# Seven passes of a two-layer kernel in one block, semaphores counted on over the passes

## The chip, the cores and the metric

The kernel runs on one core of one Trainium2 chip. The metric is the device time of one execution in microseconds; it is repeated, and the median stands for the kernel.

## The reference

Sixteen samples of 512 tokens by 256 channels, f32, go through two layers with adaptive layer norm (shift, scale and gate per sample, from a small product with the conditioning vector):

```python
mod = (_silu(L0_c) @ L0_wmod).reshape(L0_c.shape[0], 6, 1, -1)
h = _layernorm(x) * (1 + ca) + sa
x = x + ga * _L0_attn_ref(h, ...)      # 16 heads, q/k layer norm, causal softmax
h = _layernorm(x) * (1 + cb) + sb
x = x + gb * _L0_ffn_ref(h, ...)       # silu(w1 x)*(w2 x), two 1024x1024 gelu stages, w3
# layer 1, its own c and wmod
x = x + ga * _L1_attn_ref(h, ...)      # in-projection, selective scan over 512 steps, 16 states
x = x + gb * _L1_ffn_ref(h, ...)       # blocks of 32 rounded to an fp6 grid, one 256x256 product
```

## The kernel before

The work is a software pipeline over samples. A **pass** `b` has up to four parts with a flag each: `att` and `ffn` (layer 0's attention and feed-forward of sample `b`), `pre` (layer 1 of sample `b-1`: in-projection, then states 0 to 11 of the selective scan) and `fin` (sample `b-2`: the last four states, "tail", the gate, the output projection, the quantised product and the store). Passes 2 to 15 have all four and are one body in a loop `nc.Fori(2, B)`; passes 0, 1, 16 and 17 are written out around it. Pass 0 is cut in two (its attention, then a block that finds a flag, then its feed-forward, the "feed").

One pass is one call of `one_block` (L479): a block with one list of calls for each engine, interleaved by hand. TensorE, VectorE (DVE), ScalarE (ACT), GpSimd (POOL) and SyncE (SP, which loads weight tiles) meet at a block's end. After it `turn_over` (L2012) is a second block, in which POOL clears all semaphores, so each pass can count from zero; then the engines meet again and, in the loop, branch back.

```python
def one_pass(b, att, fin, pre, has_rest):
    one_block(b, att, fin, pre, att, has_rest)
    if att or pre:
        turn_over()
```

The end and the start of a pass, which the prediction speaks of:

- End, in this order on DVE: the last scan steps (L1694, L1703), `ffn_add` (L1724, reads the last product of the feed-forward), `next_scale` (L225: multiplies the centred next sample `ln_x` by its reciprocal deviation). On ACT: square, Ln, Exp of the next sample's layer norm, then `rotate_b` (L1285, copies `xa` to `xb`). On POOL: the last eight scan sums (L590). On PE: the last feed-forward product, then `next_var` (L214).
- Start: DVE `pick_mod` (L1603: copies this pass's columns of `mod` to `m0`, `m1`, `m2`; L1607 and L1610 two tiny products), then `tail_in` (L1622) and `tail_scan` (L1631), then `normalise` (L1750) for the first q/k tile. ACT `att_norm` (L1193, needs `m0` and the scaled `ln_x`, writes `h_ln`), four `tail_decay` (L1202), then `square` (L1316) of the first projection. PE `tail_spread` (L728), `pre_mean` (L208, reads `xb`), `project` (L840, reads `h_ln`). POOL `clear` (L531 to L536): a memset of two columns, of `v_pad` (128x2048), of `row_max` (128x1024), and of the ones column.

PE also carries, for each product with a weight tile, a branch over code for the weights' rounding rest (L783).

Of the kernel before, what the change touches and what calls it, by code (L numbers as in the profile page):

```python
# [40 lines left out]
SA, CA, GA, SB, CB, GB = (DC * i for i in range(6))  # L41


def build(nc, a, y_fm, x2_store=None):
    B = a["x_fm"].shape[0] - 1
    ctx = ExitStack()
    with ctx:
# [111 lines left out]
        def bank(i):  # L159
            return ps[:, i, :]  # L160
# [50 lines left out]
        def pe_var(pe, k, bk):  # L211
            pe.wait_ge(ln_sq, k)
            for c in range(DC):
                mm = pe.matmul(bank(bk), mean_mat[:, :], ln_s[:, c, :], start=(c == 0), stop=(c == DC - 1))  # L214
            mm.then_inc(ln_var, 1)

        def dve_centre(dve, src, k, bk):
            dve.wait_ge(ln_mean, k)
            if k > 1:
                dve.wait_ge(ln_out, DC * (k - 1))  # L220
            dve.tensor_tensor(ln_x[:, :, :], src[:, :, :], bcast_c(bank(bk)), ALU.subtract).then_inc(ln_cent, 1)  # L221

        def dve_scale(dve, k):
            dve.wait_ge(ln_rstd, k)
            dve.tensor_tensor(ln_x[:, :, :], ln_x[:, :, :], bcast_c(ln_s[:, 1, :]), ALU.mult).then_inc(ln_norm, 1)  # L225

        def act_square(act, k):
            act.wait_ge(ln_cent, k)
            if k > 1:
                act.wait_ge(ln_norm, k - 1)  # L230
            act.activation(ln_s[:, :, :], ln_x[:, :, :], ACT.Square).then_inc(ln_sq, 1)

        def act_rstd(act, k, bk):
            act.wait_ge(ln_var, k)
            act.activation(ln_s[:, 0, :], bank(bk), ACT.Ln, bias=eps[:, 0:1]).then_inc(ln_log, 1)
            act.wait_ge(ln_log, k)
            act.activation(ln_s[:, 1, :], ln_s[:, 0, :], ACT.Exp, scale=-0.5).then_inc(ln_rstd, 1)

        def act_affine(act, dst, k, m, scale, shift):
            act.wait_ge(ln_norm, k)  # L240
# [238 lines left out]
        def one_block(b, att, fin, pre, ffn, has_rest, first=False):  # L479
            numbers = iter(range(1, 5))  # L480
            k_pre, k_fin, k_ffn, k_next = (next(numbers) if on else None for on in (pre, fin, ffn, ffn))

            def heads_of(quad):
                return [quad // 2 * HC + 2 * g + quad % 2 for g in range(4)]

            def pair_of(v, h):
                return v[:, 2 * h:2 * h + 2, :]

            def at_of(n, m):
                return IM * (n - HEAD) + m  # L490

            def wait_tile_used(sp, r):
                if r < HM // 2:
                    sp.wait_ge(up_done, 2 * (r + 1))
                else:
                    sp.wait_ge(mid_done, r - HM // 2 + 1)

            with nc.Block() as block:
                @block.sync
                def _(sp):  # L500
                    if first:
                        split_sync(sp)
                    elif att:
                        first_tiles(sp)
                    if ffn:
                        sp.wait_ge(att_added, DC)
                        sp.dma_start(xn[:, :, :], a["x_fm"][b + 1]).then_inc(x_loaded, 16)
                        if pre:
                            sp.wait_ge(acc_init, IM)
                            sp.wait_ge(u_ready, 2)  # L510
                        with sp.If(has_rest > 0):
                            for r in range(2):
                                sp.dma_start(wrest[:, r, :].bitcast(F32), w_lo[r]).then_inc(rest_loaded[r], 16)
                        for r in range(3, FT):
                            wait_tile_used(sp, r - 3)
                            sp.dma_start(wring[:, r % 3, :].bitcast(F32), w_hi[r]).then_inc(w_loaded[r % 3], 16)
                            with sp.If(has_rest > 0):
                                if r == 3:
                                    wait_tile_used(sp, 0)
                                    sp.dma_start(wrest[:, 0, :].bitcast(F32), w_lo[2]).then_inc(rest_loaded[0], 16)  # L520
                                wait_tile_used(sp, r - 2)
                                sp.dma_start(wrest[:, r % 2, :].bitcast(F32), w_lo[r]).then_inc(rest_loaded[r % 2], 16)
                        sp.wait_ge(x_loaded, 16)
                    if fin:
                        sp.wait_ge(stored, 16)

                @block.gpsimd
                def _(pool):
                    def clear():
                        if fin or pre:  # L530
                            pool.memset(hb[:, 4:8, :].rearrange("p (a b) t -> p a b t", b=2)[:, :, 1, 0:1], 0.0).then_inc(tail_cols, 1)  # L531
                        if att:
                            pool.memset(v_pad.rearrange("p a b c -> p (a b c)"), 0.0).then_inc(pads_clear, 1)
                            pool.memset(row_max.rearrange("p a b c -> p (a b c)"), 0.0).then_inc(pads_clear, 1)
                            pool.wait_ge(pads_clear, 1)
                            pool.memset(v_pad[:, :, :, HS:HS + 1], 1.0).then_inc(ones_set, 1)  # L536

                    def causal_probs(quad, u):
                        if att:
                            for j, at in T_GROUPS[u]:  # L540
                                pool.wait_ge(exp_done, 3 * quad + u + 1)
                                blk = probs[u][:, :, at:at + P]
                                pool.affine_select(blk, blk, [[0, 4], [1, P]], ALU.is_ge, 0.0, base=0, channel_multiplier=-1).then_inc(p_masked, 1)  # L543

# [1581 lines left out]
```

## Time and profile before

| | us |
|---|---|
| median of 3 runs | 4514.94 (4514.47 to 4517.28) |
| the profiled execution's own time | 4515.7 |
| span in its trace (first to last instruction) | 4513.9 |
| busy: PE / DVE | 3731.1 / 3552.5 |
| busy: POOL / ACT | 2517.6 / 2436.1 |
| mean granted TensorE clock | 0.909 of full speed |

"Busy" counts the time in which an engine executes. The idle time in brackets on a timeline's line is that of the engine just before the line's work, with the work that seems to have ended it; "issue" means that the profile shows nothing waited for, and names ending in q are sequencers.

### The profile page before, as it was taken

To read this page: it belongs to the slowest core of one execution; us is meant where nothing else is said; L and a number is where in the kernel's file an instruction comes from. 1 tells how busy PE (TensorE), PEld (TensorE's weight loads), DVE (VectorE), ACT (ScalarE), POOL (GpSimd) and SP (SyncE) were. 2 spreads that over 40 slices of the span, in tenths; PEclk is the share of its full clock that TensorE was granted. 3 is DMA by queue.
4 is the path that set the end of the run, shared out by engine and by line. 5 is a ranking of instruction groups with operands and counts; after the bars stand their busy time and mean duration, and the time that the engine had idled before them with its cause. 6 is when DMAs were issued, how large, how long until landed. Compare 5 with 4: busy or idle time off the path is not lost. (4 is left out here: it accounts for less than half of the span.)

```text
span 4513.9 us, 51258 instructions
## 1 busy us (share of the span) xinstructions
PE 3731.1 (83%) x17261; PEld 2207.2 (49%) x17261; DVE 3552.5 (79%) x3917; ACT 2436.1 (54%) x3413; POOL 2517.6 (56%) x1895
## 2 busy tenths in 40 slices
PE   5788888889888888989888888989888888888623
PEld 3364645546464544636464554646455464645301
DVE  4514788888897888888787887879788888978895
ACT  2343555656465555646565564656555564655532
POOL 0132747557483746648474664848375574837562
PEclk8697999999999999999999999999999999999856
DMA  5530201102020211203020120303011020202000
GB/s 180 215 103 1 90 19 57 57 22 92 5 94 15 77 37 33 80 5 108 1 91 23 47 66 10 104 1 99 15 61 52 24 90 5 94 15 80 19 5 5
DMA packets 69414, 247.75 MB, mean 55 GB/s; under 512 B 9600, under 2 KB 10112, under 8 KB 68736
## 3 DMA queue, kind: packets, MB, share of 16 engines
q1 hardware_dynamic: 66816, 235.28, 15.6%
q10 hardware_dynamic: 2304, 8.39, 0.5%
q8 instruction: 204, 3.34, 0.3%
q14 instruction: 90, 0.74, 0.1%
HBM read 212.19 MB, written 31.46 MB: 54 GB/s over the span
## 5 line engine op out<-in xcount | busy, mean ns | idle before, releaser
L590 POOL TENSOR_TENSOR kept<-kept,hb 128x512 f32<-128x512 f32 x640 | 809.7, 1303 | 28.2 <-DVE hb L1703 28.2
L558 POOL TENSOR_TENSOR kept<-kept,hb 128x1024 f32<-128x1024 f32 x128 | 335.6, 2639 | 766.9 <-DVE hb L1638 694.2
L1694 DVE TENSOR_TENSOR_SCAN hb<-ps,hb 128x512 f32<-128x512 f32 x640 | 742.8, 1206 | 6.5 <-ACT ps L1227 5.6
L794 PE MATMUL ps<-hid_bhi,wring 128*128 128x512 f32 x1536 | 623.5, 406 | 17.3 <-issue 13.8
L794 PE MATMUL ps<-hid_blo,wring 128*128 128x512 f32 x1536 | 607.7, 396 | 0.0
L1227 ACT ACTIVATE ps<-kept,a_neg 128x512 f32<-128x512 f32 x640 | 431.6, 691 | 263.6 <-DVE hb L1694 263.5
L1764 DVE TENSOR_REDUCE room<-ps 128x4 f32<-128x2048 f32 (+3 forms) x256 | 375.7, 1489 | 251.3 <-PE ps L962 250.1
L543 POOL TENSOR_SCALAR_AFFINE_SELECT room<-room 128x512 f32<-128x512 f32 x256 | 224.4, 893 | 586.2 <-ACT room L1389 586.2
L794 PE MATMUL ps<-hid_ahi,wring 128*128 128x512 f32 x1280 | 514.3, 402 | 18.8 <-POOL hid_alo L605 18.4
L794 PE MATMUL ps<-hid_alo,wring 128*128 128x512 f32 x1280 | 503.5, 393 | 0.0
L1389 ACT ACTIVATE room<-ps 128x2048 f32<-128x2048 f32 (+1 forms) x192 | 305.2, 1590 | 257.7 <-PE ps L988 257.7
L1703 DVE TENSOR_TENSOR hb<-hb,ps 128x512 f32<-128x512 f32 x640 | 402.7, 677 | 16.3 <-PE ps L757 16.3
L794 PEld LDWEIGHTS ps<-hid_bhi,wring 128*128 128x128 f32 x1536 | 290.6, 189 | 118.3 <-DVE ln_s L1718 19.4
L794 PEld LDWEIGHTS ps<-hid_blo,wring 128*128 128x128 f32 x1536 | 290.6, 189 | 66.1 <-issue 3.3
L1683 DVE TENSOR_TENSOR hb<-kept,ps 128x512 f32<-128x512 f32 x480 | 306.8, 679 | 18.2 <-POOL kept L590 8.6
L960 PE MATMUL ps<-room 32*128 32x512 f32 (+3 forms) x2048 | 232.5, 526 | 71.0 <-DVE room L1771 23.6
L794 PEld LDWEIGHTS ps<-hid_ahi,wring 128*128 128x128 f32 x1280 | 240.5, 188 | 103.1 <-POOL hid_alo L605 43.5
L1631 DVE TENSOR_TENSOR_SCAN hb<-hb 128x1024 f32<-128x1024 f32 x128 | 288.9, 2279 | 1.0 <-issue 0.8
L988 PE MATMUL ps<-room 32*128 32x512 f32 (+3 forms) x2048 | 215.3, 518 | 70.4 <-DVE room L1764 54.6
L794 PEld LDWEIGHTS ps<-hid_alo,wring 128*128 128x128 f32 x1280 | 240.6, 188 | 53.1 <-issue 0.2
L757 PE MATMUL ps<-bc_parts,bc_sel 128*128 128x512 f32 x320 | 137.6, 463 | 125.5 <-DVE hb L1683 77.2
L728 PE MATMUL ps<-bc_parts,bc_sel 128*128 128x512 f32 x128 | 81.1, 633 | 172.8 <-issue 119.1
(188 smaller groups left out, 7710.7 us busy)
## 6 DMA issues: line engine op xcount, KB each, us to landing
wring<-w_hi SPq DMA_DIRECT2D x352, 512.0 KB, 3.3
kept<-in_wffn SPq DMA_DIRECT2D x22, 512.0 KB, 5.3
w_hi<-wring SPq DMA_DIRECT2D x22, 512.0 KB, 6.2
w_lo<-wrest SPq DMA_DIRECT2D x22, 512.0 KB, 3.7
xn<-in_x_fm SPq DMA_DIRECT2D x17, 512.0 KB, 3.3
out_fm<-xc ACTq DMA_DIRECT2D x16, 512.0 KB, 6.8
room<-in_wmod SPq DMA_DIRECT2D x2, 1536.0 KB, 8.1
win<-in_win SPq DMA_DIRECT2D x1, 1024.0 KB, 8.4
```

What stands on the lines that cost most here:

```text
L543: pool.affine_select(blk, blk, [[0, 4], [1, P]], ALU.is_ge, 0.0, base=0, channel_multiplier=-1).then_inc(p_masked, 1)
L558: pool.tensor_tensor(pair_of(acc, h), pair_of(acc, h), pair_of(hb, h), ALU.add).then_inc(tail_acc, 2)
L590: pool.tensor_tensor(acc[:, m, :], acc[:, m, :], hb[:, s % 8, :], ALU.add).then_inc(acc_done, 1)
L794: mm = pe.matmul(bank(bk), wring[:, r % 3, at + k * P:at + (k + 1) * P], src[i][:, k, :], start=(k == 0 and i == 0), stop=(k == K - 1 and ...
L960: pe.matmul(bank(g)[:, at:at + w], q_ver[r, p, c, i * P:(i + 1) * P], k_ver[r, p, c, 0:w], start=True, stop=False)
L1227: act.activation(bank(2 + m % 2), dt[:, m, :], ACT.Identity, bias=1.0, scale=a_neg[:, m, n:n + 1]).then_inc(a_ready, 1)
L1389: act.activation(probs[u], ps[:, 0:4, 0:G_WIDTH[u]], ACT.Exp).then_inc(exp_done, 1)
L1631: dve.tensor_tensor_scan(both, pair_of(hb, 2 + h).rearrange("p a t -> p (a t)"), both, 0.0, ALU.mult, ALU.add).then_inc(tail_scanned, 2)
L1683: dve.tensor_tensor(hb[:, s % 8, :], u[:, m, :], bank(0), ALU.mult).then_inc(b_ready, 1)
L1694: dve.tensor_tensor_scan(hb[:, s % 8, :], bank(2 + m % 2), hb[:, s % 8, :], 0.0, ALU.mult, ALU.add).then_inc(scanned, 1)
L1703: dve.tensor_tensor(hb[:, s % 8, :], hb[:, s % 8, :], bank(1), ALU.mult).then_inc(y_ready, 1)
L1764: ins = dve.tensor_reduce(cols, ps[:, 0:4, at:at + (i + 1) * P], AX.X, ALU.max, negate=True)
```

## The change

`one_block` becomes five functions, one for each engine, which take a pass as a record with the passes in front of it in the same block. `run(passes)` opens one block, and each engine goes through all the passes of the list. A target of a wait is counted on by what earlier passes of the block add to that semaphore (`since`). Where the block's end used to order two passes, waits are added at the place of first use. The lists of calls inside a pass stay in their order. The loop now has two turns of seven passes; the feed and pass 1 share a block, and so do passes 16 and 17. `turn_over` stays after each block except the last. SP's waits for the input load and the store move to the block's end.

```diff
+        def counting(p):
+            def since(signal, n):
+                earlier = 0
+                for q in p.before:
...
+                        flag, count = per_pass[signal.num]
+                        earlier += count * {"att": q.att, "ffn": q.ffn, "pre": q.pre, "fin": q.fin}[flag]
+                return earlier + n
...
+            elif att:
+                sp.wait_ge(mid_done, since(mid_done, 0))
                 first_tiles(sp)
...
             def clear():
                 if fin or pre:
+                    pool.wait_ge(acc_done, since(acc_done, 0))
                     pool.memset(hb[:, 4:8, :].rearrange("p (a b) t -> p a b t", b=2)[:, :, 1, 0:1], 0.0).then_inc(tail_cols, 1)
                 if att:
+                    pool.wait_ge(mid_done, since(mid_done, 0))
                     pool.memset(v_pad.rearrange("p a b c -> p (a b c)"), 0.0).then_inc(pads_clear, 1)
...
             def pre_mean():
                 if pre:
+                    pe.wait_ge(rotated, since(rotated, 0))
+                    pe.wait_ge(ln_cent, k_pre.number - 1)
...
             def tail_spread(which, j):
...
+                    else:
+                        pe.wait_ge(ffn_added, since(ffn_added, 0))
+                        pe.wait_ge(gelu_done, since(gelu_done, 0))
+                        pe.wait_ge(head_y, since(head_y, 0))
...
             def att_norm():
                 if att:
+                    act.wait_ge(ln_norm, sum(q.pre + q.fin + 2 * q.ffn for q in p.before))
+                    act.wait_ge(hid_split, since(hid_split, 0))
+                    act.wait_ge(mid_done, since(mid_done, 0))
...
             def pick_mod():
+                dve.wait_ge(ln_out, DC * sum(q.pre + q.fin + q.ffn for q in p.before))
+                dve.wait_ge(ffn_added, since(ffn_added, 0))
+                dve.wait_ge(out_ready, since(out_ready, 0))
+                dve.wait_ge(att_added, since(att_added, 0))
...
             def tail_in(j, h):
...
+                    else:
+                        dve.wait_ge(acc_done, since(acc_done, 0))
...
+        def run(passes):
+            with nc.Block() as block:
+                @block.sync
+                def _(sp):
+                    for p in passes:
+                        sync_pass(sp, p)
+                    for p in passes:
+                        finish(sp, p)
...
-        one_block(0, False, False, False, True, has_rest)
-        turn_over()
-        one_pass(1, True, False, True, has_rest)
-        with nc.Fori(2, B) as b:
-            one_pass(b, True, True, True, has_rest)
-        one_pass(B, False, True, True, has_rest)
-        one_pass(B + 1, False, True, False, has_rest)
+        feed = Pass(0, False, False, False, True, False, ())
+        whole_0 = Pass(0, True, False, False, True, False, ())
+        run([feed, Pass(1, True, False, True, True, False, (whole_0,))])
+        turn_over()
+        with nc.Fori(0, (B - 2) // 7) as turn:
+            steady = []
+            for i in range(7):
+                steady.append(Pass(turn * 7 + (2 + i), True, True, True, True, False, tuple(steady)))
+            run(steady)
+            turn_over()
+        last = Pass(B, False, True, True, False, False, ())
+        run([last, Pass(B + 1, False, True, False, False, False, (last,))])
```

DVE before, from the end of a pass (pass 1, the loop's first pass behind it) over the boundary:

```order
L225 TENSOR_TENSOR ln_x<-ln_x,ln_s 128x1024 [waits ln_rstd]
L498 UNCONDITIONAL_BRANCH
L2051 UNCONDITIONAL_BRANCH [waits barrier_Pool_Activation_PE_DVE_SP_release]
L1590 UNCONDITIONAL_BRANCH
L1603 ISA
L1603 COPY m<-mod 128x12
L1603 ISA
L1603 COPY m<-mod 128x12
L1603 ISA
L1603 COPY m<-mod 128x12
L1607 TENSOR_TENSOR g<-m,s 128x2 [waits mod_ready]
L1610 TENSOR_TENSOR gbias<-m,ffb 128x2
```

DVE in the changed kernel, at the boundary between two passes of one block:

```order
L228 TENSOR_TENSOR ln_x<-ln_x,ln_s 128x1024 [waits ln_rstd]
L1719 ISA [waits out_ready,att_added,ffn_added,ln_out]
L1719 COPY m<-mod 128x12
L1719 REGISTER_ALU
L1719 COPY m<-mod 128x12 x2
L1723 TENSOR_TENSOR g<-m,s 128x2 [waits mod_ready]
L1726 TENSOR_TENSOR gbias<-m,ffb 128x2
L1740 TENSOR_TENSOR hb<-kept,ps 128x1024 [waits tail_b,acc_done,mod_ready]
```

The three branches and the wait for the other engines are gone; `pick_mod`'s copies stand right behind `next_scale`, with waits on signals of other engines in front.

POOL before, the same boundary (L2017 is the clearing of the semaphores):

```order
L590 TENSOR_TENSOR kept<-kept,hb 128x512 [waits y_ready,acc_done] x8
L498 UNCONDITIONAL_BRANCH
L2015 UNCONDITIONAL_BRANCH [waits barrier_Pool_Activation_PE_DVE_SP_gather]
L2017 ISA
L2014 UNCONDITIONAL_BRANCH
L2051 UNCONDITIONAL_BRANCH [waits barrier_Pool_Activation_PE_DVE_SP_gather]
L527 UNCONDITIONAL_BRANCH
L531 MEMSET hb 128x2
L533 MEMSET room 128x2048
L534 MEMSET room 128x1024
L536 MEMSET room 128x64 [waits pads_clear]
```

POOL in the changed kernel:

```order
L668 TENSOR_TENSOR kept<-kept,hb 128x512 [waits y_ready,acc_done] x8
L608 MEMSET hb 128x2 [waits acc_done]
L611 MEMSET room 128x2048 [waits mid_done]
L612 MEMSET room 128x1024
L614 MEMSET room 128x64 [waits pads_clear]
L636 TENSOR_TENSOR kept<-kept,hb 128x1024 [waits tail_y] x2
```

The memsets of `clear` now follow the eight last sums directly.

## Rows read from the trace of the kernel before

**Rows 1.** Busy time by stretch, passes 2, 3 and 4 (from copy L1603 to copy).
```profile
core 0: us, PE busy (x) PEld busy (x) DVE busy (x) ACT busy (x) POOL busy (x), PEclk, DMA share, GB/s
585.85:842.35 256.50, 224.80 (x1072) 132.85 (x1072) 218.87 (x239) 149.90 (x211) 161.00 (x121) 0.95 0.16 52
842.35:1098.41 256.06, 224.01 (x1072) 133.18 (x1072) 216.63 (x239) 150.01 (x211) 158.23 (x118) 0.95 0.15 50
1098.41:1358.04 259.63, 227.09 (x1072) 134.68 (x1072) 217.42 (x240) 150.01 (x211) 157.35 (x119) 0.94 0.15 50
```
**Rows 2.** Timeline, boundary of passes 3 and 4: start, length, engine, line, [idle before].
```profile
1083.00 10.00 POOL L590 TENSOR_TENSOR kept<-kept,hb 128x512 f32<-128x512 f32 x8
...
1091.55 2.53 DVE L225 TENSOR_TENSOR ln_x<-ln_x,ln_s 128x1024 f32<-128x1024 f32 x1
1091.67 1.06 ACT L1285 ACTIVATE xb<-xa 128x1024 f32<-128x1024 f32 x1 [0.22 <-DVE xa L1724]
...
1095.71 1.80 POOL L533 MEMSET room<- 128x2048 f32 x1
...
1098.41 0.42 DVE L1603 COPY m<-mod 128x12 f32 x3 [4.33 <-issue]
1098.62 1.52 ACT L1193 ACTIVATE h_ln<-ln_x,m 128x512 f32<-128x512 f32 x2 [5.89 <-DVE m L1603]
...
1099.01 0.79 PE L728 MATMUL ps<-bc_parts,bc_sel 128*128 128x512 f32 x1 [8.95 <-issue]
...
1100.05 2.54 ACT L1202 ACTIVATE hb<-kept,a_neg 128x512 f32<-128x512 f32 x4
...
1102.22 4.47 DVE L1631 TENSOR_TENSOR_SCAN hb<-hb 128x1024 f32<-128x1024 f32 x2
1103.01 4.71 PE L840 MATMUL ps<-h_ln,wqk 128*128 128x512 f32 x8
...
1106.04 0.60 ACT L1316 ACTIVATE room<-ps 128x512 f32<-128x512 f32 x1 [3.45 <-PE ps L840]
...
1109.45 3.67 PE L840 MATMUL ps<-h_ln,wqk 128*128 128x512 f32 x8
...
1110.00 0.69 DVE L1750 TENSOR_TENSOR room<-ps,room 128x512 f32<-128x512 f32 x1 [3.31 <-ACT room L1327]
```
**Rows 3.** Busy time by stretch, with granted clock, at the same boundary.
```profile
1095.00:1099.00 4.00, 0.00 (x0) 0.00 (x0) 0.55 (x5) 0.38 (x1) 2.87 (x4) 0.50 0.57 198
1099.00:1103.00 4.00, 3.99 (x5) 1.84 (x6) 3.16 (x5) 3.59 (x6) 0.00 (x0) 0.50 0.55 208
```
**Rows 4.** Timeline, boundary of passes 1 and 2, reached without the loop's branch.
```profile
585.66 1.80 POOL L533 MEMSET room<- 128x2048 f32 x1
...
585.85 2.56 DVE L1603 COPY m<-mod 128x12 f32 x3 [1.54 <-PEq L2014]
...
588.42 1.52 ACT L1193 ACTIVATE h_ln<-ln_x,m 128x512 f32<-128x512 f32 x2 [5.46 <-DVE m L1603]
```
**Rows 5.** Timeline, boundary of the feed and pass 1.
```profile
323.66 1.23 DVE L225 TENSOR_TENSOR ln_x<-ln_x,ln_s 128x1024 f32<-128x1024 f32 x1 [2.34 <-ACT ln_s L237]
...
326.19 1.84 DVE L1603 COPY m<-mod 128x12 f32<-128x12 f32 x2 [1.30 <-PEq L2014]
...
327.93 0.99 POOL L534 MEMSET room<- 128x1024 f32 x1
328.06 1.52 ACT L1193 ACTIVATE h_ln<-ln_x,m 128x512 f32<-128x512 f32 x2 [3.48 <-DVE m L1603]
328.08 0.16 DVE L1607 TENSOR_TENSOR g<-m,s 128x2 f32<-128x2 f32 x1
```
**Rows 6.** Timeline, boundary of passes 16 and 17.
```profile
4407.99 0.10 POOL L531 MEMSET hb<- 128x2 f32 x1 [1.28 <-POOLq L2014]
...
4408.94 2.35 DVE L1622 TENSOR_TENSOR hb<-kept,ps 128x1024 f32<-128x1024 f32 x2 [0.54 <-PE ps L728]
```
**Rows 7.** The line of PE's branches over the rest code: count, ns, first and last.
```profile
L783 PEldq COMPARE_BRANCH  x544: 202/208/369, 232.2 to 4196.0; - x182
```

More of the change, by code:

```diff
@@ L1 @@
+from collections import namedtuple
 from contextlib import ExitStack
@@ L41 @@
 SA, CA, GA, SB, CB, GB = (DC * i for i in range(6))
+Norm = namedtuple("Norm", "number outs")
+Pass = namedtuple("Pass", "b att fin pre ffn first before")
 def build(nc, a, y_fm, x2_store=None):
@@ L477, in build @@
         BODY = NS - TAIL - HEAD
[L479 to L494, printed above, removed]
-                else:
-                    sp.wait_ge(mid_done, r - HM // 2 + 1)
+        UNITS = 3 * HM + DC
@@ new lines, in build, with each @@
+        BODY = NS - TAIL - HEAD
+        per_pass = {}
+        def each(flag, n, *signals):
+            for x in signals:
+                per_pass[x.num] = (flag, n)
+        each("att", 1, ones_set)
+        each("att", 2, att_in, v_done, v_copied, pads_clear, att_out, att_added)
+        each("att", 4, qk_done, qk_squared, qk_summed, qk_logged, qk_rstd_ready, qk_normed, ver_even, ver_odd, max_turned, q_shifted,
+             o_copied, o_summed, o_inverted, o_spread, o_turned, o_normed)
+        each("att", 3 * QUADS, s_done, max_ready, st_done, exp_done, pv_done)
@@ new lines, in build @@
+        each("att", 4 * QUADS, p_masked)
+        each("ffn", HM, up_done, gate_ready, gated_up, up_rounded)
+        each("ffn", 2 * HM + DC, mid_done)
+        each("ffn", 4 * HM, gelu_done)
+        each("ffn", 3 * HM, hid_split)
+        each("ffn", DC, ffn_added, h_rounded, h_split)
+        each("ffn", 16, x_loaded)
+        for i in range(3):
+            each("ffn", 16 * len(range(i, FT, 3)), w_loaded[i])
+        for i in range(2):
+            each("ffn", 16 * len(range(i, FT, 2)), rest_loaded[i])
@@ L500, in _ @@
                 def _(sp):
[L501 to L523, printed above, removed]
@@ L833, in project @@
-                    def project(i):
-                        if att:
-                            pe.wait_ge(att_in, DC)
-                            if i >= 2:
-                                pe.wait_ge(qk_logged, i - 1)
-                            m = i // 2 + DC * (i % 2)
-                            for c in range(DC):
-                                mm = pe.matmul(bank(i), wqk[:, c, m * P:(m + 1) * P], h_ln[:, c, :], start=(c == 0), stop=(c == DC - 1))
-                            mm.then_inc(qk_done, 1)
@@ L1171, in _ @@
[L1171 to L1180 removed]
+                    for p in passes:
+                        tensor_pass(pe, p)
                 @block.scalar
                 def _(act):
[L1184 to L1187 removed]
@@ L2005, in _ @@
-                    times_c(11, 0)
-                    scan(11, 1)
-                    times_c(11, 1)
-                    ffn_add(0)
-                    ffn_add(1)
-                    next_scale()
+                    for p in passes:
+                        vector_pass(dve, p)
         def turn_over():
```

2848 lines of the change are left out of this document (1484 added, 1364 removed).

## Prediction

> **What bounds the kernel now.** I read the busy time pass by pass first. The pass from 1098.41 us lasts 259.63 us, and in it PE is busy 227.1, DVE 217.4, POOL 157.4 and ACT 150.0 [rows 1]. No engine fills the pass: it is a chain that runs from engine to engine in the order written by hand, and whatever stands still for all of them adds directly. So I then read the timeline where two passes meet, to see how long all of them stand still. DVE ends `next_scale` at 1091.55 + 2.53 = 1094.08, POOL its last sum at 1093.00, ACT `rotate_b` at 1092.73, and PE has been idle for 8.95 us when it starts again at 1099.01 [rows 2]. Nothing but POOL's memsets runs between 1094.08 and 1098.41 [rows 2]. Third, the granted clock of this stretch: 0.50 both while PE stands still (1095 to 1099) and when it works again (1099 to 1103) [rows 3], the lower of the two levels, 1.2 GHz. Eight matmuls of `project` take 4.71 us there and 3.67 us one group later [rows 2].
>
> What follows the gap is the chain `m0` copy, `att_norm`, `project`, `square`, `normalise`: ACT starts `att_norm` at 1098.62 and its first `square` at 1106.04; DVE, which has finished its scans 3.31 us earlier, starts `normalise` at 1110.00 [rows 2]. The first thing to ask is therefore how much earlier `square` comes.
>
> A measurement of this kernel can tell a change of about 0.2%, 9 us, from none.
>
> **The change, part by part.** Of the boundaries between passes, twelve of the loop (2 to 3 up to 7 to 8, 9 to 10 up to 14 to 15) lose both meetings, the clearing and the branch back, and so do two others (feed to 1, 16 to 17). The ones behind passes 1, 8 and 15 stay.
>
> *DVE, the copies.* They can start at 1094.1. I look for what is in their way. POOL's `clear` now follows its last sum at once, so its memsets (before: 1095.71 to 1098.54) run from 1093.1 to about 1096.0, under the copies. Where a copy met them in the trace, it was held: three copies took 2.56 us and not 0.42, and `att_norm` started 588.42 - 585.66 = 2.76 us after the large memset [rows 4]; at the feed's boundary 328.06 - 326.19 = 1.87 us after it [rows 5]. (There the memset of 1.80 us starts with the copy.) From a large memset at 1093.15 these give an `att_norm` at 1095.9 or 1095.0; I take the middle, 1095.5. Free copies would give 1094.08 + 0.21 = 1094.3. So `att_norm` comes 1098.62 - 1095.5 = 3.1 us earlier, with bounds of 2.7 and 4.3.
>
> *ACT.* `att_norm` takes 1.52 and the four `tail_decay` behind it 2.54 us [rows 2]: ACT is free for `square` at 1095.5 + 4.1 = 1099.6.
>
> *PE.* `tail_spread` and `pre_mean` wait for `ffn_add` and for `rotate_b`'s end at 1092.73; four matmuls at the rate of the faster group (3.67/8 each) end at 1094.6, well before `att_norm` ends at 1097.0. Then the first four matmuls of `project` are done at 1097.0 + 1.9 = 1098.9, before ACT is free, and all eight at 1100.7 where they ended at 1107.72. `square` starts at 1099.6 and not at 1106.04: **6.4 us earlier**; the second projection is 7.0 earlier, which leaves 6.4 as the smaller.
>
> *DVE again.* With the copies done at about 1095.8, `tail_in` (2.3 us) ends at 1098.1, `tail_scan` (4.47 us) waits for its second decay (1097.0 + 1.27) and ends at 1102.8 [rows 2]. `normalise` is due at 1110.00 - 6.4 = 1103.6. DVE's slack falls from 3.31 to 0.8 us, but it doesn't decide.
>
> *Costed at nothing.* The added waits are for signals of 1093 or earlier, in front of instructions that start later. SP's first weight tiles are loaded earlier; they are needed only by the feed-forward, over 100 us on. The end-of-pass waits of SP and the extra register work stand beside the 1.4 us in which DVE waits for POOL. If that cover is gone they cost some tenths.
>
> *The two others.* Feed to 1: `next_scale` ends at 324.89, POOL is long free, so `att_norm` starts at 325.1 and not at 328.06: 3.0 us [rows 5]. 16 to 17: POOL's last sum ends at 4407.99 - 1.28 = 4406.7, and `tail_in`, now behind a wait for it, starts at 4406.8 and not at 4408.94: 2.1 us [rows 6].
>
> *Sum.* 12 x 6.4 + 3.0 + 2.1 = 81.9 us, against the profiled execution's own 4515.7 us: 4433.8. The median of the runs is 0.8 us lower than the profiled one, so I write **4433 us**.
>
> **Two rules against the rows.** The copies are held while memsets run [rows 4, 5], but `g3`, a product with two inputs in SBUF, takes its usual 0.16 us under the memset of 327.93 [rows 5]. I take from this that `next_scale`, which has two such inputs and is 2.53 us long behind POOL's sums against 1.23 us without them [rows 2, 5], waits for the sums and not for the memsets behind them. The Trainium skill says the same (SBUF — State Buffer, section "SBUF: two separate sides"): the port pair that DVE and GpSimd share is an exclusive lock, and a DVE operation with two SBUF inputs meets it only against a GpSimd operation that reads SBUF. By that rule the trace agrees in both points; without it, the fourth case below would weigh more.
>
> DVE was idle 4.33 us before the loop's pass and 1.54 us before one reached in straight code [rows 2, 4]: the branch back costs 2.8 us of the gap. The Trainium skill (Runtime: NRT & Kernel Launch, section "Instruction fetch mechanics") says that fetching is purely sequential and that a taken branch out of what is fetched stalls. A rule on the length of code, which would speak against 7 passes written out, is not in it.
>
> **The rivals.**
>
> *A clock that still falls, or a step lost elsewhere.* Passes 2 and 3 took 256.50 and 256.06 us, pass 4 259.63, with the same counts of instructions and PE busy 224 to 225 against 227 us [rows 1]: a pass comes in steps of about 3.4 us, by where in it the clock is low. Between 1090.1 and 1097.0 PE would have only some 2.3 us of work, so the clock may fall all the same. One step worse in the twelve passes is +12 x 3.4 = 41 us: 4474; half of that (low only under the projections) gives 4453.
>
> *A step won, or free copies.* If the copies get in before the memset, ACT's chain is 1.2 us shorter: 12 x 1.2 = 14, 4419. One clock step better gives 4433 - 41 = 4392. For it: PE's long idle stretch is gone. Against: the other low stretches of the pass are untouched.
>
> *The memsets hold `next_scale`.* It would start at 1096.0 and end at 1097.3; `att_norm` at 1097.5 is 1.1 us earlier: 4515 - 12 x 1.1 - 5 = 4497. Against it, `g3` [rows 5].
>
> *Slower: code that arrives late.* Place: PE's 544/16 = 34 branches in each pass [rows 7], taken over code that is not run. Price: the 2.8 us that the branch back costs. It decides from 6.4/2.8 = 2.3 stalls a pass on; at one in ten branches a pass loses 9.5 - 6.4 = 3.1 us, and the kernel takes 4515 + 12 x 3.1 - 5 = 4547 us. Against: these branches take 0.2 us [rows 7], and pass 2, the loop's first turn, run when its code had never run, was not longer than pass 4 [rows 1].
>
> *The change doesn't do what it says.* If one of the added waits makes an engine wait for the last of all the others, only the branch and the clearing go: the 2.8 us at most, which ends near 4480, or nothing at all if it is made up by waits: 4515.
>
> **How the numbers follow.** Forecast (held copies, clock mostly high) 0.50; step lost, whole or half, 0.20; step won or free copies 0.20; memsets hold `next_scale` 0.04; waits that keep the meeting 0.03; late code 0.03. The forecast's own bounds are 2.7 to 4.3 us at `att_norm`, that is 12 x 0.4 = 5 us up and 14 us down: 4419 to 4438. To leave out no more than 2 in 10 the range reaches down into the won step and up to nearly all of the lost one: 4400 to 4470. Faster by over 0.2%: 0.95; within: 0.02; slower: 0.03.
>
> **What would show it.** In the changed profile, at an inner boundary: DVE's `pick_mod` (L1719) starts within 0.2 us of `next_scale`'s end but lasts 1 to 2 us, with POOL's memsets (L611, L612) beside it; `att_norm` (L1296) starts 1.4 us after `next_scale` ends, the first `square` (L1421) 5.5 us after it where it was 12.0; granted clock above 0.9 in the 10 us behind `next_scale`; a pass takes 253 us; the boundaries at the loop's head are as before. It is wrong if the passes get no shorter than 256 us, if the clock is at 0.50 under `project`, or if idle time by "issue" appears on PE inside a pass.

## The result, and the profile after

| | before | changed |
|---|---|---|
| median, us (4 runs each, taken together) | 4514.7 | 4409.64 (4406.64 to 4410.43) |
| ratio to before | | 0.9767, interval 0.975 to 0.9784 |
| the profiled execution's own time | 4515.7 | 4410.43 |
| span in its trace | 4513.9 | 4408.7 |
| mean granted TensorE clock | 0.909 | 0.919 |

The change makes the kernel faster by 105 us. The forecast was 4433 us, which is 82 us of gain. Its range (4400 to 4470) holds the result; the gain was 23 us larger than the sum.

From the page of the changed kernel: its span, the engines' busy time, the clock in 40 slices (tenths of full speed), the two queues that fetch instructions (packets, MB), and the largest group of matmuls of the feed-forward with the idle time in front of it.

```profile
span 4408.7 us, 51342 instructions
...
PE 3700.5 (84%) x17261; PEld 2188.9 (50%) x17261; DVE 3558.4 (81%) x3917; ACT 2435.4 (55%) x3413; POOL 2530.8 (57%) x1895
...
PEclk8697999999999999999999999999999999999856
...
q8 instruction: 186, 3.05, 0.3%
q14 instruction: 130, 1.06, 0.1%
...
L881 PE MATMUL ps<-hid_bhi,wring 128*128 128x512 f32 x1536 | 623.2, 406 | 17.3 <-issue 13.8
```

PE's busy time fell from 3731.1 to 3700.5 us with the same work, which is the clock; the other three engines' busy times are within 15 us of before: for them the gain is idle time. The pass table, with the columns of [rows 1], for passes 4 and 9 of the changed kernel (pass 9 stands behind the loop's turn, which kept its meetings):

```profile
1086.66:1336.05 249.39, 222.06 (x1073) 132.42 (x1072) 217.95 (x241) 149.88 (x211) 159.65 (x119) 0.97 0.16 52
2344.91:2599.44 254.53, 228.17 (x1076) 135.25 (x1077) 219.48 (x240) 150.00 (x211) 158.24 (x119) 0.95 0.17 57
```

Before, passes 2 to 4 took 256.50, 256.06 and 259.63 us [rows 1]. Pass 4 now takes 249.39: 10 us less, where the forecast had 6.4. So the next thing to read is where in the pass they went. This is the timeline of the changed kernel where passes 4 and 5 meet, with the columns of [rows 2]:

```profile
1333.58 2.54 DVE L228 TENSOR_TENSOR ln_x<-ln_x,ln_s 128x1024 f32<-128x1024 f32 x1
...
1333.71 0.49 PE L815 MATMUL ps<-bc_parts,bc_sel 128*128 128x512 f32 x1 [1.63 <-DVE xa L1842]
...
1334.80 1.98 PE L212 MATMUL ps<-xb,mean_mat 128*128 128x512 f32 x4 [0.59 <-ACT xb L1389]
...
1335.13 1.80 POOL L611 MEMSET room<- 128x2048 f32 x1
...
1336.05 0.94 DVE L1719 COPY m<-mod 128x12 f32 x3
1336.87 1.00 POOL L612 MEMSET room<- 128x1024 f32 x1
1337.05 0.16 DVE L1723 TENSOR_TENSOR g<-m,s 128x2 f32<-128x2 f32 x1
1337.08 1.52 ACT L1296 ACTIVATE h_ln<-ln_x,m 128x512 f32<-128x512 f32 x2 [2.33 <-DVE m L1719]
...
1338.51 2.54 ACT L1307 ACTIVATE hb<-kept,a_neg 128x512 f32<-128x512 f32 x4
...
1338.65 3.70 PE L933 MATMUL ps<-h_ln,wqk 128*128 128x512 f32 x8 [1.86 <-ACT h_ln L1296]
...
1340.02 4.47 DVE L1749 TENSOR_TENSOR_SCAN hb<-hb 128x1024 f32<-128x1024 f32 x2 [0.30 <-ACT hb L1307]
...
1340.95 0.57 ACT L1421 ACTIVATE room<-ps 128x512 f32<-128x512 f32 x1
...
1344.63 0.69 DVE L1868 TENSOR_TENSOR room<-ps,room 128x512 f32<-128x512 f32 x1
```

`next_scale` (L228) ends at 1333.58 + 2.54 = 1336.12. I count from there, since before the change PE's, ACT's and DVE's first work of the new pass all stood behind that end, and give "before" from [rows 2] counted from its own 1094.08. DVE's copies (L1719) stand at -0.07 us (before +4.33), `att_norm` (L1296) at +0.96 (before +4.54), the first `project` (L933) at +2.53 (before +8.93), `square` (L1421) at +4.83 (before +11.96), `normalise` (L1868) at +8.51 (before +15.92). PE starts `tail_spread` (L815) and `pre_mean` (L212) 2.4 and 1.3 us before `next_scale` ends. `g` (L1723), the product with two inputs in SBUF, takes its 0.16 us under the memset L612, and `next_scale` takes 2.54 us as before. The clock there, for comparison with [rows 3]:

```profile
1334.00:1338.00 4.00, 2.19 (x5) 0.68 (x4) 3.85 (x7) 1.67 (x3) 3.94 (x5) 1.00 0.43 166
1338.00:1342.00 4.00, 3.35 (x8) 1.63 (x9) 3.70 (x3) 3.52 (x6) 0.03 (x1) 1.00 0.00 0
```

It is 1.00, 2.4 GHz, where it was 0.50 before. In all, the start of a pass is 7.4 us shorter. The rest of the pass is the other part. These are pass 4 of the kernel before and pass 4 of the changed one, each from `normalise` to the end of the next `next_scale`:

```profile
1110.00:1353.45 243.45, 216.10 (x1055) 130.05 (x1053) 210.02 (x230) 143.50 (x201) 154.34 (x114) 0.96 0.14 46
```

```profile
1095.25:1336.12 240.87, 215.40 (x1059) 129.96 (x1058) 210.01 (x231) 143.49 (x201) 157.73 (x116) 0.96 0.16 53
```

243.45 us became 240.87, although nothing in this stretch was changed: the counts of DVE (230, 231) and ACT (201) are the same but for one record, and their busy times too. What differs is where in it the clock is low. The 8 us that begin 44 us behind `normalise`, before and changed:

```profile
1154.00:1162.00 8.00, 6.28 (x20) 3.27 (x21) 5.93 (x6) 1.58 (x3) 6.17 (x5) 0.65 0.00 0
```

```profile
1139.20:1147.20 8.00, 6.21 (x29) 3.01 (x33) 7.30 (x7) 1.75 (x4) 6.10 (x5) 1.00 0.00 0
```

The kernel before runs at 0.65 of full speed here, the changed one at 1.00; the next `split_bc`, which ends this stretch, comes 64.28 us behind `normalise` before and 60.97 us in the changed kernel. That is 3.3 us; 0.7 of them are lost again further on in the pass. Over the twelve inner boundaries the time from `next_scale`'s end to `normalise` fell from a mean of 15.89 to 8.95 us, and the rest of the pass from 243.28 to 241.87: together 8.35 us a pass, 12 x 8.35 = 100 of the 105 us of span.

Two of the twelve boundaries, in front of passes 8 and 15, are not like the others. Here is the one in front of pass 8, where `next_scale` ends at 2085.11 + 2.54 = 2087.65:

```profile
2086.66 1.80 POOL L611 MEMSET room<- 128x2048 f32 x1
...
2087.57 1.83 DVE L1719 COPY m<-mod 128x12 f32 x3
...
2089.49 1.52 ACT L1296 ACTIVATE h_ln<-ln_x,m 128x512 f32<-128x512 f32 x2 [3.22 <-DVE m L1719]
...
2091.07 5.40 PE L933 MATMUL ps<-h_ln,wqk 128*128 128x512 f32 x8 [2.75 <-ACT h_ln L1296]
...
2098.74 0.69 DVE L1868 TENSOR_TENSOR room<-ps,room 128x512 f32<-128x512 f32 x1 [1.83 <-ACT room L1432]
```

And the stretch in it in which the granted clock is low:

```profile
2091.70:2095.10 3.40, 3.40 (x6) 1.32 (x5) 3.10 (x3) 2.36 (x4) 0.00 (x0) 0.50 0.00 0
```

The copies stand behind both memsets (1.83 us instead of 0.94), `att_norm` is at +1.84, and PE has been idle for 2.75 us when it starts `project`. It starts at the higher clock (1.00 until 2091.70), and 0.6 us later the clock falls to 0.50 for 3.4 us: the eight matmuls take 5.40 us and not 3.70. `normalise` comes at +11.09, 2.6 us later than in the ten others. In front of pass 15 PE is idle for 2.90 us, and the clock falls 1.2 us into `project`. And where the loop turns, in front of pass 9, the gap is as it was before, and a little longer (`next_scale` ends at 2339.65; the copies stand at +5.26, and PE's idle time is 9.95 us where it was 8.95 in [rows 2]):

```profile
2337.12 2.53 DVE L228 TENSOR_TENSOR ln_x<-ln_x,ln_s 128x1024 f32<-128x1024 f32 x1
...
2344.91 2.49 DVE L1719 COPY m<-mod 128x12 f32 x3 [5.27 <-issue]
...
2345.58 0.76 PE L815 MATMUL ps<-bc_parts,bc_sel 128*128 128x512 f32 x1 [9.95 <-issue]
```

### The profile page after: what moved, and what is told of

Read it like the earlier page. It is cut to its first block and busy times, and to the rows that moved or that the text cites. A ratio compares the mean times of both kernels' runs of the same rounds, so it can differ in the third digit from the quotient of the medians.

```text
span 4408.7 us, 51342 instructions
## 1 busy us (share of the span) xinstructions
PE 3700.5 (84%) x17261; PEld 2188.9 (50%) x17261; DVE 3558.4 (81%) x3917; ACT 2435.4 (55%) x3413; POOL 2530.8 (57%) x1895
## 5 line engine op out<-in xcount | busy, mean ns | idle before, releaser
L881 PE MATMUL ps<-hid_bhi,wring 128*128 128x512 f32 x1536 | 623.2, 406 | 17.3 <-issue 13.8
L881 PE MATMUL ps<-hid_blo,wring 128*128 128x512 f32 x1536 | 608.0, 396 | 0.0
L621 POOL TENSOR_SCALAR_AFFINE_SELECT room<-room 128x512 f32<-128x512 f32 x256 | 237.8, 945 | 570.8 <-ACT room L1498 570.8
L881 PE MATMUL ps<-hid_ahi,wring 128*128 128x512 f32 x1280 | 514.4, 402 | 18.7 <-POOL hid_alo L683 17.9
L881 PE MATMUL ps<-hid_alo,wring 128*128 128x512 f32 x1280 | 503.5, 393 | 0.0
L881 PEld LDWEIGHTS ps<-hid_bhi,wring 128*128 128x128 f32 x1536 | 290.6, 189 | 117.8 <-DVE ln_s L1836 19.2
L881 PEld LDWEIGHTS ps<-hid_blo,wring 128*128 128x128 f32 x1536 | 290.5, 189 | 66.6 <-issue 3.3
L881 PEld LDWEIGHTS ps<-hid_ahi,wring 128*128 128x128 f32 x1280 | 240.5, 188 | 103.1 <-POOL hid_alo L683 43.2
L881 PEld LDWEIGHTS ps<-hid_alo,wring 128*128 128x128 f32 x1280 | 240.6, 188 | 53.1 <-issue 0.2
L844 PE MATMUL ps<-bc_parts,bc_sel 128*128 128x512 f32 x320 | 138.4, 465 | 122.7 <-DVE hb L1801 74.4
L683 POOL TENSOR_TENSOR hid_alo<-ln_s,hid_ahi 128x512 fp32r<-128x512 f32 x128 | 166.0, 1305 | 86.7 <-ACT hid_ahi L1369 77.0
```

Of the source, the lines that this page charges most:

```text
L881: mm = pe.matmul(bank(bk), wring[:, r % 3, at + k * P:at + (k + 1) * P], src[i][:, k, :], start=(k == 0 and i == 0), stop=(k == K - 1 and ...
```

## The experiments

Savings below are against the runs of the kernel before on the same chip (medians 4511.24, 4513.42 and 4516.9 us in the three series). The intervals of the ratios are some 0.0015 to each side, 7 us, so a difference between two experiments is read together with the traces. All diffs are against the changed kernel.

**Which part of the boundary costs what.** The first experiment keeps seven passes written out in a turn, but each in a block of its own and with its `turn_over`, semaphores counted from zero each time: only the branch back is gone.

```diff
-            steady = []
             for i in range(7):
-                steady.append(Pass(turn * 7 + (2 + i), True, True, True, True, False, tuple(steady)))
-            run(steady)
-            turn_over()
+                run([Pass(turn * 7 + (2 + i), True, True, True, True, False, ())])
+                turn_over()
```

> Seven passes a turn, but each in its own block with both meetings and the clearing behind it, so that only the branch back is gone from the twelve inner boundaries. Theory A (three parts: branch back, meetings, overlap): at the boundary of passes 1 and 2 of the kernel before, which has no branch back, the first square came 592.29 - 584.31 = 8.0 us behind next_scale and not 12.0, so 4.0 of the 7.1 us that the first square gained at an inner boundary are the branch: about 4409.6 + 12 x 3.1 = 4447 us. Rival B (the meetings and the clearing are what costs, the branch is hidden behind the memsets that hold the copies): att_norm gains only 4.5 - 4.1 = 0.4 us, and the time stays above 4490.

Measured: 4444.69 us, 0.9855 (0.9839 to 0.9872), a saving of 66.6 us. The second keeps one meeting, at the end of each block, and counts the semaphores on, without clearing.

```diff
-            run(steady)
+                run([steady[-1]])
```

> As e1, but the semaphores are counted on over the seven passes and not cleared between them: one meeting at an inner boundary instead of two. Theory A: the second meeting starts 0.9 us after the first in the trace of before (1094.4 and 1095.3), so 12 x 0.9 = 11 us less than e1: about 4436. Rival C (what matters is that any meeting keeps PE idle and lets the clock fall, not how long it is): same as e1 within 5 us, granted clock 0.50 at the boundary in both.

Measured: 4434.84 us, 0.9837 (0.9821 to 0.9853), a saving of 76.4 us. The third has the code of the change, but one pass in a turn: branch, meetings and clearing are all back at the twelve boundaries, and gone at the two outer ones (feed to 1, 16 to 17).

```diff
-        with nc.Fori(0, (B - 2) // 7) as turn:
+        with nc.Fori(0, (B - 2)) as turn:
...
-            for i in range(7):
+            for i in range(1):
```

> The changed kernel with one pass a turn: only feed and pass 1, and passes 16 and 17, share a block. The prediction's two last terms alone: 3.0 + 2.1 us, 4514.7 - 5.1 = 4509.6. If the added waits cost anything inside a pass it shows here as more than 4510, since nothing of the inner boundaries is gained.

Measured: 4511.67 us over 10 runs against 4511.24 over 13 of the kernel before, 1.0001 (0.9991 to 1.0011). The 5.1 us forecast for the outer boundaries are not seen, though the interval, some 4.5 us to each side, excludes them only just. By the time alone, added waits that cost about as much as these boundaries give would look the same. Its trace speaks against that: counted from one `next_scale` to the next, the passes behind the twelve boundaries take 259.39 us in the mean against 259.17, and without the first of them 259.41 against 259.43. So the added waits and the register work cost nothing that can be seen in a pass. Both outer boundaries are shorter in the trace (the feed's by 3.3 us to `normalise`), and pass 3 is 2.9 us longer than the same pass before (259.26 against 256.32). Its span, 4509.6 us, is still 4.3 below that of the kernel before. Why the medians on one chip don't differ stays open.

So, per inner boundary and by the runs: the branch back 66.6/12 = 5.6 us, the second meeting with the clearing (76.4 - 66.6)/12 = 0.8, the last meeting (105.1 - 76.4)/12 = 2.4. The middle one is within the intervals, the first and the last are beyond them. This charges all of a saving to the twelve boundaries, and the first experiment has the shorter outer ones too. The means of the passes behind these boundaries in the traces (259.17 us before, then 254.57, 252.64 and 250.83) leave that out. They give 4.6 us for the branch back, 1.9 for the second meeting (1.5 of it before `normalise`) and 1.8 for the last. The timeline of the first experiment, in front of pass 5, shows what a boundary with two meetings and no branch is:

```profile
1339.30 2.53 DVE L228 TENSOR_TENSOR ln_x<-ln_x,ln_s 128x1024 f32<-128x1024 f32 x1
...
1343.27 0.77 PE L815 MATMUL ps<-bc_parts,bc_sel 128*128 128x512 f32 x1 [5.46 <-PEq L2164]
...
1343.42 1.55 DVE L1719 COPY m<-mod 128x12 f32 x3 [1.60 <-PEq L2164]
1343.83 3.62 PE L212 MATMUL ps<-xb,mean_mat 128*128 128x512 f32 x4
...
1347.24 4.71 PE L933 MATMUL ps<-h_ln,wqk 128*128 128x512 f32 x8
...
1354.23 0.69 DVE L1868 TENSOR_TENSOR room<-ps,room 128x512 f32<-128x512 f32 x1 [1.74 <-ACT room L1432]
```

```profile
1342.00:1346.00 4.00, 2.73 (x4) 1.50 (x5) 2.43 (x6) 0.93 (x2) 2.92 (x4) 0.58 0.49 164
```

The copies stand 1.59 us behind `next_scale`'s end at 1341.83, as in [rows 4] and not 4.33 as in [rows 2]: this is the 2.8 us of the branch. PE, idle for 5.46 us, comes back at 0.58 of full speed, and its four `pre_mean` matmuls take 3.62 us and eight `project` 4.71 us. Most passes in this trace take 252.7 or 255.9 us: the shorter ones start with a low stretch of 3.4 us that is over before `project`, the longer ones with one of 6.8 us that reaches into it. Half of the difference stands before `normalise` (10.8 against 12.4 us), the other half in the rest of the pass.

Two passes in a turn leave seven inner boundaries in place of twelve.

```diff
-        with nc.Fori(0, (B - 2) // 7) as turn:
+        with nc.Fori(0, (B - 2) // 2) as turn:
...
-            for i in range(7):
+            for i in range(2):
```

> The changed kernel with two passes a turn: 7 inner boundaries instead of 12. Theory A (each inner boundary is worth the same 7.9 us): 4409.6 + 5 x 7.9 = 4449 us. Rival D (much of the gain is a state of the clock that a row of passes settles into): further off, above 4460 or below 4435, with the passes behind an inner boundary not near 251 us.

Measured: 4454.66 us, 0.9873 (0.9853 to 0.9893): a saving of 56.6 us, 8.1 for each of seven inner boundaries where the change has 105.1/12 = 8.8. The gain goes with the number of boundaries. (Four of the seven in its trace are of the kind in which the copies stand behind both memsets, `normalise` at +11.1; in the change it is two of twelve.) And no loop at all, all passes in one block:

```diff
-        run([feed, Pass(1, True, False, True, True, False, (whole_0,))])
-        turn_over()
-        with nc.Fori(0, (B - 2) // 7) as turn:
-            steady = []
-            for i in range(7):
...
-            run(steady)
-            turn_over()
-        last = Pass(B, False, True, True, False, False, ())
-        run([last, Pass(B + 1, False, True, False, False, False, (last,))])
+        line = [Pass(1, True, False, True, True, False, (whole_0,))]
+        for b in range(2, B + 2):
+            att = b < B
+            line.append(Pass(b, att, True, b <= B, att, False, (whole_0, *line)))
+        run([feed, *line])
```

> No loop: the feed and all passes 1 to 17 in one block, 17 passes counted on. The three boundaries left (1 to 2, 8 to 9, 15 to 16) go too. Theory A: 8.0 us less at each straight one is too much, since no branch was there: 8.0 - 4.9 = 3.1 us for two of them and 8 for the loop's: about 4409.6 - 14 = 4395. Rival E (code that was never run comes late, or longer code costs): 4410 or more, with idle time by issue inside passes.

Measured: 4398.73 us, 0.9751 (0.9736 to 0.9766), a saving of 114.7 us, 10 more than the change. By the intervals alone this is not told from the change; its span, 4397.0 us against 4408.7, agrees. It also bears on the rival of late code, since every pass is code that runs for the first time. From its page, the queues that fetch instructions:

```profile
q8 instruction: 185, 3.03, 0.3%
q14 instruction: 121, 0.99, 0.1%
```

It fetches 185 + 121 packets where the changed kernel fetches 186 + 130 and the one before 204 + 90: longer code is not fetched more, and passes 2 to 15, none of them run before, take 249.3 to 252.4 us where the changed kernel's passes behind an inner boundary take 249.3 to 252.0.

**The clock.** The forecast took a clock that stays up for granted and gave 0.20 to a lost step. This experiment moves only PE's work at the boundary: the first `tail_spread` waits for the first of DVE's copies, so that PE stands still until then, as it did with a meeting.

```diff
                         pe.wait_ge(head_y, since(head_y, 0))
+                        if p.before:
+                            pe.wait_ge(mod_ready, since(mod_ready, 1))
```

> The changed kernel, but PE's tail_spread and pre_mean of the next pass also wait for the copy of m0, so PE stands still for some 5 us at an inner boundary, as long as it did in part of the old gap. Clock theory: the granted clock falls to 0.50 there and project runs at half rate; the first square comes 5.4 us or more behind next_scale, and the pass is 2 to 4 us longer: 4434 to 4457 us. Rival (the clock at the boundary is worth nothing, since ACT is what square waits for): the added wait alone delays the eight matmuls of project by 0.9 us: 4410 to 4420.

Measured: 4433.79 us, 0.9826 (0.981 to 0.9842): a saving of 79.6 us, 25.5 less than the change. In front of pass 5 of its trace:

```profile
1327.45 2.55 DVE L228 TENSOR_TENSOR ln_x<-ln_x,ln_s 128x1024 f32<-128x1024 f32 x1
...
1329.92 0.95 DVE L1721 COPY m<-mod 128x12 f32 x3
...
1330.98 0.71 PE L817 MATMUL ps<-bc_parts,bc_sel 128*128 128x512 f32 x1 [5.04 <-DVE m L1721]
...
1331.49 3.36 PE L212 MATMUL ps<-xb,mean_mat 128*128 128x512 f32 x4
...
1334.68 3.60 PE L935 MATMUL ps<-h_ln,wqk 128*128 128x512 f32 x8
...
1340.56 0.69 DVE L1870 TENSOR_TENSOR room<-ps,room 128x512 f32<-128x512 f32 x1 [1.93 <-ACT room L1434]
```

```profile
1330.00:1334.00 4.00, 3.02 (x4) 1.46 (x5) 3.20 (x7) 3.04 (x5) 1.90 (x3) 0.63 0.00 0
```

`next_scale` ends at 1330.00, and the copies and `att_norm` stand where the changed kernel has them (-0.08, +0.96). But PE has been idle for 5.04 us, comes back at the lower level (0.63 in this stretch), and takes 3.36 us for the four `pre_mean` matmuls that take 1.98 in the changed kernel; `project` has to stand behind them, at +4.68 and not +2.53, and `normalise` comes at +10.56 and not +8.51. This delay is not the clock alone, since PE also starts later. An estimate of the shares: at the rate that these matmuls have in the next experiment's rows (0.31 us from `tail_spread` to `pre_mean`, 1.88 us for the four) `pre_mean` would end at 1330.98 + 0.31 + 1.88 = 1333.17, and it ends at 1334.85. So the clock makes some 1.7 of the 2.15 us by which `project` comes later, and the late start the rest. Over the twelve boundaries the passes of this trace are 1.7 us longer than in the changed kernel (252.54 against 250.83 us), 21 of the 25.5 us. (Its profiled execution, 4421 us, was the shortest of its four; the others lie at 4432.4 to 4435.3. Its pass 1 is 8 us shorter than in the trace of the changed kernel.)

The reverse: the kernel with both meetings, and PE given four extra products in front of them. Their result is written to a bank that nothing reads.

```diff
+                    if fin and pre:
+                        for _ in range(4):
+                            pe.matmul(bank(6), mean_mat[:, :], xn[:, 0, :], start=True, stop=True)
```

> As e1 (own block, both meetings), with four more f32 products of 128x512 on PE behind next_var, whose result nothing reads: about 3.5 us of work in the time in which PE stands still and waits for the others. In e1 the start of a pass comes in two lengths, 10.8 us and 12.4 us from next_scale to normalise, granted clock low for 3.4 or 6.8 us. Clock theory: with PE idle for some 2 us only, the clock stays at 1.00 there, every start is 10.8 us, 12 x 0.9 = 11 us less than e1 or more if the rest of the pass follows: about 4434. Rival (the low clock beside the meetings costs nothing, the lengths differ for another reason): 4445 as e1, or more if the added work delays the meeting.

Measured: 4433.35 us, 0.9806 (0.9793 to 0.982): a saving of 83.5 us against 66.6 without the extra work, beyond the intervals. In front of pass 4 of its trace:

```profile
1088.55 0.47 PE L815 MATMUL ps<-bc_parts,bc_sel 128*128 128x512 f32 x1 [2.05 <-PEq L2167]
...
1088.86 1.88 PE L212 MATMUL ps<-xb,mean_mat 128*128 128x512 f32 x4
...
1091.92 3.70 PE L936 MATMUL ps<-h_ln,wqk 128*128 128x512 f32 x8 [1.19 <-ACT h_ln L1299]
```

The meeting is there (PE's idle time ends with its sequencer at the block's end, L2167), but that time is 2.05 us and not 5.46, and `pre_mean` and `project` run at the rate of the higher level, 1.88 and 3.70 us. So part of what two meetings cost is the clock behind them: 0.8 us a boundary by the traces' means from `next_scale` to `normalise` (11.72 without, 10.94 with the extra products), 1.4 by the savings (16.9/12). It doesn't work in every pass: in front of pass 5 of this trace PE comes back from 2.06 us of idle time, and the granted clock is 0.50 from 1340.2 to 1343.6.

**The memsets.** `clear` waits until DVE's copies are done:

```diff
                     pool.wait_ge(mid_done, since(mid_done, 0))
+                    pool.wait_ge(mod_ready, since(mod_ready, att + pre + fin))
                     pool.memset(v_pad.rearrange("p a b c -> p (a b c)"), 0.0).then_inc(pads_clear, 1)
```

> The changed kernel, but POOL's memsets of v_pad and row_max wait for the copies, so that nothing holds the copies. In the changed kernel the three copies take 0.94 us and not 0.42, and att_norm starts 1.03 us behind next_scale. Held-copies theory: att_norm starts 0.3 us behind it, 0.7 us earlier, and 12 x 0.7 = 8 us go: 4401. Rival (the memsets now hold tail_in or normalise of DVE, or come too late for copy_v): nothing gained or up to 10 us lost.

Measured: 4393.73 us, 0.9739 (0.9725 to 0.9754): a saving of 119.7 us, 15 more than the change. The two intervals just touch, so the trace has to decide. In front of pass 5:

```profile
1328.59 2.52 DVE L228 TENSOR_TENSOR ln_x<-ln_x,ln_s 128x1024 f32<-128x1024 f32 x1
...
1331.04 0.31 DVE L1720 COPY m<-mod 128x12 f32 x3
1331.31 1.52 ACT L1297 ACTIVATE h_ln<-ln_x,m 128x512 f32<-128x512 f32 x2 [1.55 <-DVE m L1720]
...
1331.47 1.80 POOL L612 MEMSET room<- 128x2048 f32 x1 [1.28 <-DVE m L1720]
...
1338.86 0.69 DVE L1869 TENSOR_TENSOR room<-ps,room 128x512 f32<-128x512 f32 x1
```

The copies take 0.31 us, `att_norm` stands at +0.20, `normalise` at +7.75. That is 0.76 us less than in the ten boundaries of the changed kernel in which the copies got in between the memsets, and 3.3 to 3.5 less than in the two in which they didn't; all twelve are alike here. The passes behind them take 249.15 us in the mean and not 250.83. `next_scale` takes 2.52 us with no memset beside it: the memsets never held it.

**Both together.** No loop, and `clear` behind the copies, by the diffs of these two experiments and nothing else:

> e4 and e5 together: no loop, one block from the feed to the end, and the memsets behind the copies. If their gains add: 4409.6 - 15.9 - 10.9 = 4383 us, and 15 passes of one length, 249 us. If the clock's steps decide: anywhere from 4378 to 4400.

Measured: 4373.56 us (4369.15 to 4377.43), 0.9682 (0.9668 to 0.9695). This is the fastest version, 143 us under the kernel before and some 38 under the change. The two alone gave 15 and 10, so by the medians there are some 14 us more than their sum. That is hardly outside what the intervals of three ratios leave open, and the spans of the profiled executions don't show it: 4408.7 becomes 4388.8 with the late `clear` and 4397.0 without the loop, 19.9 and 11.7 us, and 4375.7 with both, 33.0 us. So the two gains add up, and more than that is not shown. All its fourteen passes of this kind start like the twelve of the experiment on the memsets (means of 7.77 and 7.75 us to `normalise`), and the mean granted clock of its execution is 0.925 against 0.922 and 0.918 with one of the two alone.

## Why the prediction was right, and where it was off

**What bounds the kernel: right.** A chain with all engines standing still between passes. The first two experiments and the change take the boundary apart, and the passes get shorter with each part that goes.

**`att_norm`, 3.1 us earlier: too little.** Seen in ten of twelve boundaries: 4.54 - 0.96 = 3.6 us. The middle between 1095.0 and 1095.9 was taken because copies had been seen held by memsets; they are, but in ten boundaries only by the first (+0.96 where the forecast had +1.4), in two by both (+1.84, +1.99, outside the forecast's upper bound). The lower bound of the two was the better value. 4.3 us, the free copies, came only with the experiment on the memsets.

**`square` 6.4 us earlier: 7.1 in ten boundaries, 5.3 to 5.7 in the two others.** The steps of PE went as written, with `project` 1.57 us behind `att_norm`'s start. The distance from `att_norm` to `square` was taken as 4.1 us, the sum of 1.52 and 2.54, and measured 3.87: each of ACT's groups starts 0.1 us before the end shown for the one ahead of it.

**`normalise`, the end that decides: the step that was mis-sized.** The forecast stopped at `square` and gave the same 6.4 us to `normalise`. It came 7.4 us earlier in the ten boundaries (15.92 to 8.51), 4.7 to 4.8 in the two, 6.94 in the mean: 12 x 6.94 = 83.3 us where the sum had 12 x 6.4 = 76.8. The 1.0 us by which the ten differ from the forecast are 0.5 at `att_norm`, 0.2 from there to `square`, and 0.3 behind `square`: there the kernel before still ran the rest of the first `project` at the lower clock (3.96 us from `square` to `normalise`, now 3.68), and I had compared `square`'s start alone.

**DVE's slack falls from 3.31 us to 0.8: right in kind, too small a fall.** The scans end at 1340.02 + 4.47 = 1344.49, 0.14 us before `normalise` starts, so DVE's chain is now as long as the one over ACT and PE. Both begin at the copies. That fits what the experiment on the memsets gave: `att_norm` 0.76 us earlier, and `normalise` 0.76 us earlier.

**The clock, a won step: a rival that came true in part.** The rest of a pass got 1.40 us shorter in the mean, 17 us in twelve: from 243.4 to between 240.8 and 241.8 in eight passes, and not at all in the other four (243.3 to 243.4). The prediction had this as a case of its own with steps of 3.4 us in every pass (4392); what came is under half of it, and it is the larger part of the 23 us by which the sum fell short. That the boundary's clock matters is shown from both sides, by the late PE (25.5 us lost, by the estimate above most of it to the clock) and the busy PE (17 us won). Why the low stretch 44 us into the pass goes when the boundary changes was only read from the traces; no run changed that stretch alone.

**The outer boundaries, 5.1 us: there in the trace, open in the time.** `att_norm` of pass 1 comes 0.20 us behind `next_scale` where it came at 3.17, and `tail_in` of pass 17 starts 0.13 us behind POOL's last sum where it was 2.23: 3.0 and 2.1 us, as forecast. 105.2 us of span less the 100 of the twelve passes leave 5 us for all the rest of the changed kernel, which would fit; the experiment that has them alone finds none in its time.

**Costed at nothing: right.** With one pass a turn the new waits and the register work give 1.0001, and passes as long as before.

**The rivals that fell.** Memsets that hold `next_scale`: it takes 2.54 us with them and 2.52 without. Late code: PE's idle time by "issue" in front of L881 is 13.8 us over the whole span, the same as before, and the version without a loop is no slower. Here the Trainium skill says, in the section cited in the prediction (Runtime: NRT & Kernel Launch, "Instruction fetch mechanics"), that the sequencer streams straight code by itself, and that a taken branch out of the fetched window stalls, which is one reason to unroll. The trace agrees in that the branch back costs 4.6 to 5.6 us a pass; that this time is spent on fetching is not shown. Waits that keep the meeting: the copies start 0.07 us before `next_scale`'s modelled end. The price that this rival had, 2.8 us at most and near 4480, was too small: the first experiment takes away the branch back alone and ends at 4445.

**In sum:** 83.3 us at the starts and 17 in the rest of the passes make 100, with 5 outside them; the forecast had 77, nothing, and 5.

## What to carry to other kernels

Where a chain of engines ends at a block's end, read the idle time of every engine around it, and then split it: the branch back, the meeting with its clearing, and the clock at which PE comes back are three prices, and here the branch was the largest. Follow the saving to the last instruction of the chain that is decided there (`normalise`, not `square`), since a stretch that ran at the lower clock gives back more than its start moves. And once the meeting is gone, work that it had kept apart (here POOL's memsets and DVE's small copies) runs together; moving the work that nobody waits for behind the copies was worth 15 us more.

## What the runs showed of the hardware that was not expected

- The loop's branch back cost 5.6 us a pass by the runs (66.6/12) and 4.6 by the passes of the traces, up to twice the 2.8 us by which DVE's idle time differs. DVE is not the engine that decides there: with the branch gone PE's idle time falls by 3.5 us (8.95 to 5.46), some passes meet the higher clock under `project`, and the mean from `next_scale` to `normalise` falls from 15.9 to 11.7 us.
- Of two memsets that stand in POOL's queue back to back, three small copies of DVE got in after the first in ten boundaries and after the second in two. The same section of the Trainium skill as in the prediction (SBUF — State Buffer, "SBUF: two separate sides") says that whichever starts first has the port pair for the whole instruction; the trace agrees for each memset.
- PE came back at 2.4 GHz from idle times of 1.86 and 2.05 us (the changed kernel, and the one with extra products), and was at 1.2 GHz from the start, or all but the start, when it came back from 5.04 and 5.46 us in the experiments. From 2.75 and 2.90 us, in front of passes 8 and 15, it came back at 2.4 GHz and the clock fell 0.6 and 1.2 us later. Idle times so near each other don't settle it: after 2.06 us, in front of pass 5 of the version with extra products, the clock fell as PE came back. In front of passes 8 and 15 copies that were 0.9 and 1.0 us late made `normalise` 2.6 and 2.7 us late.
- A pass takes one of a few lengths (256 or 259.6 before, 252.7 or 255.9 with two meetings), so a saving of a few us elsewhere, as the 5 us at the outer boundaries, is of the size of one such step.
